# Attention stage of a one-layer language-model tower: in TensorE's macro step, the sums of the values are moved from behind the other items to directly behind the two score blocks

## What is computed

```python
h = tok(x, tok_weight)                    # gather rows, quantise and dequantise them in blocks of 64
h = h + attention(layernorm(h), W_Q, b_Q, W_K, b_K, W_V, b_V, W_O, b_O)
h = h + experts(layernorm(h), ...)        # routed small experts

# attention: 12 heads of 64, causal
q, k, v = (x @ W + b for each head)
scores = q @ k.T / 8, masked above the diagonal
pattern = softmax(scores)
out = sum over heads of (pattern @ v) @ W_O + b_O
```

## Time and profile before

| | us |
|---|---|
| median of 3 runs | 2651.92 |
| the profiled execution, its own time | 2648.46 |
| its span, from the first to the last instruction | 2646.7 |
| units 0 to 10 of attention, from the first s2 of unit 0 to that of unit 11 | 295.4 to 1694.3 |
| unit 11 of attention | 1694.3 to about 1800 |

### The profile page before, as it was taken

One profiled execution on the slowest core, in us unless ns is written; L12 is line 12 of the kernel. 1 busy time (PEld: TensorE's weight loads), 2 busy tenths in 40 slices (PEclk: granted clock), 3 DMA queues, 4 the chain that ended last, 5 costly groups with the idle time before them and its releaser, 6 DMA issues. The chain is left out here.

```text
span 2646.7 us, 42215 instructions
## 1 busy us (share of the span) xinstructions
PE 2390.5 (90%) x16000; PEld 1225.3 (46%) x16000; DVE 1859.5 (70%) x3771; ACT 1231.6 (47%) x1728; POOL 1242.6 (47%) x858
## 2 busy tenths in 40 slices
PE   3565899999999999999999999996999999999998
PEld 1233555555555555555555556543333333333332
DVE  7864565656565656566565656687988989888987
ACT  3422233333333333333333333354777777777776
POOL 5000265756575757575756666663413323324120
PEclk9787899999999999999999999996999999999999
DMA  1002000000001000000000001131011000000000
GB/s 50 12 23 61 1 8 8 3 9 1 10 1 33 1 10 1 10 1 10 1 9 1 3 1 20 19 53 55 9 19 21 15 19 21 15 19 9 19 7 7
DMA packets 42940, 39.33 MB, mean 15 GB/s; under 512 B 26865, under 2 KB 35186, under 8 KB 41842
## 3 DMA queue, kind: packets, MB, share of 16 engines
q1 hardware_dynamic: 40608, 31.18, 5.3%
q0 software_dynamic: 1536, 3.15, 0.4%
q10 hardware_dynamic: 594, 2.31, 0.2%
HBM read 26.13 MB, written 10.49 MB: 14 GB/s over the span
## 5 line engine op out<-in xcount | busy, mean ns | idle before, releaser
L678 POOL TENSOR_TENSOR acc<-acc,pT 128x1024 f32<-128x1024 f32 (+3 forms) x412 | 836.0, 2029 | 239.7 <-ACT pT L1077 202.9
L1077 ACT ACTIVATE pT<-banks 128x1024 f32<-128x1024 f32 x480 | 406.7, 896 | 812.9 <-PE banks L751 747.2
L1806 DVE TENSOR_TENSOR hw<-hid,banks 128x512 f32<-128x512 f32 x1024 | 662.8, 680 | 84.0 <-PE banks L1489 69.6
L896 DVE TENSOR_REDUCE part<-banks 128x2 f32<-128x1024 f32 (+3 forms) x432 | 438.0, 1044 | 313.0 <-PE banks L727 311.3
L1648 ACT ACTIVATE hid<-banks 128x1024 f32<-128x1024 f32 x512 | 496.7, 1022 | 183.8 <-PE banks L1479 167.4
L767 PE MATMUL banks<-pT,v 128*64 128x512 f32 (+3 forms) x1920 | 405.5, 543 | 1.1 <-POOL pT L662 1.1
L1489 PE MATMUL banks<-wT,select 64*128 64x512 f16 x1024 | 341.6, 392 | 42.1 <-DVE hw L1806 22.5
L1479 PE MATMUL banks<-zst,w1c 50*128 50x512 f32 x1024 | 306.5, 541 | 10.7 <-ACT hid L1648 10.7
L1497 PE MATMUL banks<-hw,w 128*32 128x512 f32 x2048 | 278.3, 616 | 0.8 <-DVE hw L1806 0.8
L1489 PEld LDWEIGHTS banks<-wT,select 64*128 64x128 f16 x1024 | 93.7, 94 | 399.1 <-DVE hw L1806 340.2
L767 PEld LDWEIGHTS banks<-pT,v 128*64 128x64 f32 x1920 | 116.7, 136 | 203.1 <-issue 181.1
(11 more groups left out here) (228 smaller groups left out, 3161.4 us busy)
## 6 DMA issues: line engine op xcount, KB each, us to landing
zst<-z_scratch SPq DMA_DIRECT2D x48, 128.0 KB, 4.0
z_scratch<-zp SPq DMA_DIRECT2D x8, 512.0 KB, 2.8
out_h<-o SPq DMA_DIRECT2D x8, 384.0 KB, 2.6
xT_scratch<-xs_hi SPq DMA_DIRECT2D x4, 512.0 KB, 2.7
xt_hi<-xT_scratch SPq DMA_DIRECT2D x2, 1024.0 KB, 5.7
w<-in_L_ffn_W ACTq DMA_DIRECT2D x1, 2048.0 KB, 8.5
xt_hi<-in_L_ffn_W SPq DMA_DIRECT2D x12, 128.0 KB, 4.6
v<-in_L_ffn_W SPq DMA_DIRECT2D x12, 128.0 KB, 4.3
```

What stands on the lines that cost most here:

```text
L678: pool.tensor_tensor(acc[:, G % 2, :, off:CH], acc[:, G % 2, :, off:CH], pT[:, slot, :, 0:w], ALU.add).then_inc(summed, 1)
L896: last = dve.tensor_reduce(to[:, :, c:c + 1], both[:, :, 0:whole], AX.X, ALU.max)
L1077: act.activation(pT[:, J % PSLOTS, :, 0:CH - off], both[:, :, 0:CH - off], ACT.Exp, scale=E ** -0.5)\
L1806: dve.tensor_tensor(hw[:, n % 2, q, :], hid[:, n % 2, q, :], ring_bank(("w", g, n, q)), ALU.mult).then_inc(mixed, 1)
```

## The change

In TensorE's list for a macro step, the two calls of `weigh` (for the two key blocks of the step before) move from behind the step's other items to ahead of them. The order of the ring, the lists of the other engines, the number of instructions and the transfers stay as they are. A total stays at the end of its step.

```diff
                 for t in range(MACROS):
                     score_columns(it, 2 * t)
                     score_columns(it, 2 * t + 1)
-                    for item in PLAN[it][t]:
-                        side(item)
                     if t:
                         weigh(it, 2 * t - 2)
                         weigh(it, 2 * t - 1)
                     elif it:
                         weigh(it - 1, NK - 2)
                         weigh(it - 1, NK - 1)
+                    for item in PLAN[it][t]:
+                        side(item)
                     if behind(it, t, 1):
                         add_up(*behind(it, t, 1))
```

## The result

The changed kernel took 2778.79 us (median of 4 runs, 2775.79 to 2779.95), the kernel before beside it 2651.76: 1.048 times the time, 95% interval 1.0463 to 1.0499. Forecast were 2712, range 2664 to 2735. The sign was right, the loss is twice the forecast's (+127 for +60), and the time lies outside the range.

A forecast was written before the change was run, and what follows sets the result against it. TensorE was taken as the bound. Per unit, -2.3 + 1.1 + 2.1 + 4.65 = +5.55 us, with units 0 and 11 adjusted +59.7 in all, gave 2712 us, 2.3% slower; range 2664 to 2735.

The forecast's parts named there:

- term 3: Step 3: a score block waits 0.7 for k's bank, a sum 1.3 for normalise, 0.1 restart: +2.1 us a unit.
- steps 5 and 6: First-pass blocks wait for banks behind VectorE's small blocks, invert, normalise and maxima: +1.3 us a unit.
- 12 and 13: Waits of 0.43 for step 11's first block, 0.2 for the total, 0.1 in step 13, and restarts: +0.9 us.
- 19 and 0: Step 19 and the next step 0: waits at small score blocks and the rows item, plus restarts: +1.8 us.
- term 4: First-pass blocks directly ahead of score blocks make TensorE wait for banks from VectorE: +4.65 us a unit.
- Term 1: First-pass blocks find their exponentials done; of 3.1 us of waits, 2.3 us a unit are gained.
- Net 0: Step 9: the "out" keeps its 1.4 us wait; VectorE's chain starts 1.8 us later, but sums are already done.
- upper bound of 7.5 us a unit: Case of a CAST long each time and waits that do not overlap: 7.5 us a unit, 2733 us.
- less likely still that the clock would fall: TensorE's clock falling in longer waits: ranked below the rivals, without its own chance or size.
- Term 2: TensorE's switches between score and f32 matmuls: three more round trips at 0.36, 1.1 us a unit.
- steps 14 and 15: Block, maxima and invert of step 13 push step 14's three blocks back: +0.65 us, CAST taken at 1.0.
- VectorE's lateness accumulates: Rival: lateness grows from step to step and becomes the bound, 7.5 us a unit and over, 2735 to 2750; chance 0.08.

The follow-up runs named there:

- experiment 3: Kernel before, with the sums of the values ahead of the other items in step 3 alone: 2662.99 us, ratio 1.0047.
- experiment 5: Changed kernel, with all four of VectorE's small operations on a chunk's maxima written as tensor_reduce: 2712.61 us, ratio 1.024.
- experiment 4: Changed kernel, with the old order kept in steps 8, 9, 13, 14 and 15: 2717.24 us, ratio 1.0249.
- Experiments 1: Changed kernel, with only the CAST copy replaced by a second tensor_reduce: 2768.57 us, 1.045 times before.
- 8: Changed kernel, with GpSimd's running additions cut to 64 of up to 512 queries of each head: 2703.93 us, ratio 1.0200.
- experiment 7: Changed kernel, with zero-weight filler matmuls on TensorE in its two longest waits, steps 9 and 15: 2753.35 us, ratio 1.0397.
- 6: Kernel before, with the four small VectorE operations written as tensor_reduce: 2641.22 us, ratio 0.997.

## Why the prediction was wrong

**Right.** The direction; step 3 (term 3, +2.1; measured +1.65 in after, +1.9 in step 3 by itself; experiment 3, where step 2 keeps its order and so only the second of the two waits can appear: +1.5 a unit); steps 5 and 6, 12 and 13, 19 and 0 of term 4, each within 0.5 us; the stages ahead of attention and behind it, within 2 us. Unit 11 is not among them: +3.8 instead of +0.8. With the small operations out of GpSimd's way the changed order takes 2712.6 us where 2712 were forecast (experiment 5), and without the five steps of the chains 2717 (experiment 4). Such closeness is partly luck: the errors of terms 1 and 4 below have opposite signs.

**The step that failed first: VectorE's small operations were taken at a fixed length.** Term 1 said of step 9 "Net 0", and term 4 took the CAST of step 13 at 1.0 us because "1.57 there against a mean of 0.66" had been read as a spread. It was no spread: the copy ends when GpSimd's addition ends. A change that moves VectorE's chain by 1.8 us against GpSimd's list moves where in an addition of 2.4 us the copy falls. It fell on the end (0.60) and now falls on the beginning (2.07); the copy that the prediction counts to step 13 (it runs in step 14) went from 1.57 to 2.25, and in step 0 the subtraction went from 0.18 to 0.94, there held by GpSimd's copy (L675). That the same eight values took 1.57 us against a mean of 0.66 stood in the rows before, and in the trace they took 0.18 to 1.57; the question to ask was who else was at work in the long one. Experiments 1, 5 and 8 show it: change the form of one operation and the next one waits; change the form of all, or shorten GpSimd's work, and 66 us and more are gone. The upper bound of 7.5 us a unit was made with the 1.57 seen once, not with the addition's whole length, and so did not hold the truth.

**The second: the clock.** The prediction called it less likely still that the clock would fall, since 1.4 us of waiting had left it at 1.00, and gave it no chance and no price. Behind 2.65 us in step 9 and 1.78 in step 15 (unit 5) it fell, in 18 stretches of units 0 to 10; experiment 7 puts the price at about 25 us, 2.8 a unit in steps 9, 10 and 15. That in step 15 it fell in seven of eleven units only shows in the lengths: unit 5, where it fell twice, takes 139.5, unit 8, where it fell once, 137.9. The trace of the kernel before had a warning that its rows do not show: in step 0 of unit 0 TensorE waited 1.91 us for the maxima, and the clock fell behind it. The length of a wait does not settle it: waits of 1.42 to 1.60 in step 9 (the kernel before and experiment 4) left the clock at 1.00 in all units, while the wait of 1.2 in step 3, which comes soon behind one of 0.5, was followed by a fall in 7 of 60 units (units 1 to 10 of the kernel after and of experiments 1, 4, 5, 7 and 8). Why in these units and not in others, no run here shows. The Trainium skill's TensorE: Matmul & The Clock Gate, section HAM oscillation — how this bites in real kernels, tells of a loop whose wait throttles the clock anew in each round; the stretches at 0.53 and 0.56 agree with it in kind, though in step 15 not in each round.

**Term 1 was mis-sized as well.** The 3.1 us by which first-pass blocks waited for exponentials were read from the weight loads; the list of before had the matmuls' own row beside it, with 0.5:

```profile
PEld banks L727 <- ACT pT L1077: 3.1, 11, 0.5
...
PE banks L727 <- ACT pT L1077: 0.5, 2, 0.3
```

Loads run ahead, so what a load waits a matmul need not. Of the 2.3 us taken, the gaps between first-pass blocks, and between a rows item and the block behind it, show 1.25 (summed over a unit, experiment 5 against 6), and the blocks themselves, the first of which now stands behind sums, got 0.7 longer. The last line of the table (+0.4 for -1.2) is in part this. Term 2 no run tells apart. Term 4 erred the other way: without holds, steps 14 and 15 lose nothing where 0.65 were charged.

**In sum**, of the +127 us: about 61 are the forecast's own terms (2712.6 against 2651.8, the errors above and unit 11 among them), 41 the holds, 25 the clock, each good to some 3 us. That VectorE's lateness accumulates, the rival with 0.08, named a time nearer the truth (2735 to 2750) for a reason that isn't the one: VectorE is busy 78 of 139.5 us, and idles.

## What to carry to other kernels

Here an instruction whose duration varied while its shape did not was waiting inside: find which other engine's instruction ends with it before you move either, and price the move by that instruction's whole length. Read a wait from the row of the matmuls, not from that of their weight loads, and where a change gives TensorE a new wait or a longer one, give the fall of the clock a chance and a price; that one wait in the profile left it at full is no proof. An order is worth what it does to the list of the engine that comes next, two steps on; the gain here came from moving one consumer away from its chain and taking a cheap form for four small operations.

## What was not expected of the hardware

A copy of 128 x 8 values took up to 2.27 us while GpSimd added, and a subtraction of the same size up to 2.04, while a tensor_reduce over 128 x 40 took 0.20 in the same place. Replacing one held instruction wins little: of 66 us to be had, 10. And the fallen clock, which in units 0 to 10 of the kernel before came only once, in unit 0, cost more than the growth of the wait that brought it: 1.1 us in step 9 and 0.6 in step 10, behind a wait that had grown by 1.2.
